# One reciprocal standard deviation for two lanes, in place of one per lane, in a four-layer token tower

## The reference

```python
h = tok(x, W)                              # rows of the table, 0 where the id is 0
h = h + attn0(_layernorm(h), ...)          # decayed linear attention
h = h + ffn0(_layernorm(h), ...)           # 16 experts, the best 2, then a layer norm with gamma, beta
h = h + attn1(_layernorm(h), ...)          # softmax over 8 positions, two heads
h = h + ffn1(_layernorm(h), ...)           # 32 experts, the best 1
h = h + attn2(_layernorm(h), ...)          # linear attention (elu), two layer norms, gelu
h = h + ffn2(_layernorm(h), ...)           # 8 experts, the best 2, gelu
h = h + attn3(_layernorm(h), ...)          # complex diagonal recurrence
h = h + ffn3(_layernorm(h), ...)           # binary gated weights

def _layernorm(x, axis=-1, eps=1e-05):
    m = jnp.mean(x, axis=axis, keepdims=True)
    v = jnp.var(x, axis=axis, keepdims=True)
    return (x - m) / jnp.sqrt(v + eps)
```

## Time and profile before

| | |
|---|---|
| runs | 1108.0, 1112.93, 1113.48 us; median 1112.93 |
| span of the profiled execution (first to last instruction) | 1110.5 us; a time of its own is not given |
| instructions | 12887 |
| pass one, pass two (first work of VectorE) | from 39.5 us, from 580.6 us |
| busy: TensorE matmul / weight load | 956.3 us (86%) / 686.4 us (62%) |
| busy: VectorE / ScalarE / GpSimd | 580.2 us (52%) / 362.3 us (33%) / 359.3 us (32%) |
| mean granted TensorE clock | 0.717 of full speed |
| DMA | 8.01 MB in 7687 packets, nearly all in the setup |

### The profile page before, as it was taken

The page is one execution under the profiler, slowest core; times in us unless marked ns, Lnnn a source line. Parts: engine busy times, 40 slices in busy tenths (PEclk is TensorE's granted clock), DMA queues, the critical chain, the costliest instruction groups (busy, mean ns, idle before and its releaser), DMA issues. The chain is left out here.

```text
span 1110.5 us, 12887 instructions
## 1 busy us (share of the span) xinstructions
PE 956.3 (86%) x4368; PEld 686.4 (62%) x4380; DVE 580.2 (52%) x1892; ACT 362.3 (33%) x654; POOL 359.3 (32%) x418
## 2 busy tenths in 40 slices
PE   0498999989996869979959899998999965997997
PEld 0276999776675537763316689987677643586332
DVE  6344226854226663467863622487421567427787
ACT  2115431121111332019941254211200222400896
POOL 6511347431101720476002114574110064028600
PEclk9999997555555557559975599865555555856898
DMA  6000000000000000001000000000000000000520
GB/s 174 9 1 1 1 1 1 1 1 0 1 1 1 1 1 1 0 1 20 1 22 1 0 1 1 1 1 1 1 1 1 0 1 0 1 1 1 14 6 20
DMA packets 7687, 8.01 MB, mean 7 GB/s; under 512 B 5513, under 2 KB 6122, under 8 KB 7466
## 3 DMA queue, kind: packets, MB, share of 16 engines
q0 software_dynamic: 1536, 1.58, 2.5%
q1 hardware_dynamic: 5746, 4.27, 1.5%
q10 hardware_dynamic: 336, 1.31, 0.4%
HBM read 5.90 MB, written 1.25 MB: 6 GB/s over the span
## 5 line engine op out<-in xcount | busy, mean ns | idle before, releaser
L626 POOL TENSOR_SCALAR var_eps<-stat 128x4 f32<-128x4 f32 x88 | 24.7, 280 | 498.3 <-DVE stat L1173 498.3
L942 PEld LDWEIGHTS psB<-k,hid 128*128 128x128 f32 x1024 | 127.8, 201 | 4.1
L844 ACT ACTIVATE hid<-psA 128x512 bf16<-128x512 f32 x256 | 126.0, 989 | 1.0 <-PE psA L1127 1.0
L942 PE MATMUL psB<-k,hid 128*128 128x64 f32 x1024 | 125.4, 282 | 0.0
L1494 DVE TENSOR_TENSOR hid<-hid 128x512 bf16<-128x512 bf16 x256 | 108.8, 426 | 18.4 <-ACT hid L844 2.5
L859 PE MATMUL psA<-kc,xn 128*64 128x128 f32 x256 | 60.4, 405 | 66.1 <-DVE xn L1184 66.0
L765 ACT ACTIVATE hid<-psA,k 128x512 f32<-128x512 f32 x128 | 79.9, 687 | 98.8 <-PE psA L869 98.7
L629 POOL TENSOR_TENSOR inv_std<-var_eps,neg_half 128x4 f32<-128x4 f32 x88 | 95.4, 1084 | 7.3
L868 PE MATMUL psA<-xs,up_hi 128*128 128x512 f32 x176 | 89.0, 506 | 2.9 <-DVE gTb L1374 1.1
L859 PEld LDWEIGHTS psA<-kc,xn 128*64 128x64 f32 x256 | 37.2, 161 | 85.7 <-DVE xn L1184 72.6
L1127 PE MATMUL psA<-gTb,w_rows 128*128 128x512 bf16 x252 | 85.3, 383 | 3.7 <-DVE gTb L1485 1.3
(11 more groups left out here) (269 smaller groups left out, 1756.9 us busy)
## 6 DMA issues: line engine op xcount, KB each, us to landing
hid<-wup SPq DMA_DIRECT2D x2, 512.0 KB, 11.4
out<-h SPq DMA_DIRECT2D x8, 128.0 KB, 1.9
k<-w ACTq DMA_DIRECT2D x1, 972.5 KB
hid<-binary SPq DMA_DIRECT2D x1, 608.0 KB
hid<-wup SPq DMA_DIRECT2D x2, 270.0 KB, 13.5
emb<-emb_w,ids_next POOLq DMA_INDIRECT x32, 3.4
kc<-consts SPq DMA_DIRECT2D x1, 384.5 KB, 7.4
emb<-emb_w,ids_sb POOLq DMA_INDIRECT x16, 5.3
```

Source lines behind the costliest of these rows:

```text
L844: act.activation(sg[l][:, p % 2, :], psA[l][:, :], ACT.Sign).then_inc(m3_s[g], 1)
L942: last = pe.matmul(psB[l][:, to:to + D], tile(hid[l][:, e % 4, :], t), k128[:, a:a + D], start=True, stop=True)
```

## The change

A group's eight variances get one add and one power on 128x8, where each lane's four had their own. The GpSimd step yields once, at the place that lane 1 had, waits for lane 1's `norm_var`, and counts each semaphore up by 2. VectorE's program is the same; its two multiplies still wait for the counts 1 and 2 of each norm, which now come together. `neg_half` gets eight columns.

```diff
@@ -208,7 +208,7 @@
         stat = per_group("stat", [P, GROUP_TILES, 2])
         var_eps = per_group("var_eps", [P, GROUP_TILES])
         inv_std = per_group("inv_std", [P, GROUP_TILES])
-        neg_half = sb("neg_half", [P, TILES])
+        neg_half = sb("neg_half", [P, GROUP_TILES])
@@ -620,14 +620,13 @@
                         def rstd(at, use):
 
-                            for l in own:
-                                yield at + RSTD + LATER * (l - own[0])
-                                pool.wait_ge(norm_var[g], nth(l, use))
-                                G.tensor_scalar(part(var_eps[g], l), part(stat[g], l)[:, :, 1], LN_EPS, None,
-                                                ALU.add).then_inc(norm_eps[g], 1)
-                                pool.wait_ge(norm_eps[g], nth(l, use))
-                                G.tensor_tensor(part(inv_std[g], l), part(var_eps[g], l), neg_half[:, :],
-                                                ALU.pow).then_inc(norm_rstd[g], 1)
+                            yield at + RSTD + LATER
+                            pool.wait_ge(norm_var[g], nth(own[-1], use))
+                            G.tensor_scalar(var_eps[g][:, :], stat[g][:, :, 1], LN_EPS, None,
+                                            ALU.add).then_inc(norm_eps[g], GROUP_LANES)
+                            pool.wait_ge(norm_eps[g], nth(own[-1], use))
+                            G.tensor_tensor(inv_std[g][:, :], var_eps[g][:, :], neg_half[:, :],
+                                            ALU.pow).then_inc(norm_rstd[g], GROUP_LANES)
```

## The result

| | before | after |
|---|---|---|
| median of the runs | 1113.2 us (4 runs, 1108.0 to 1127.54) | 1131.12 us (4 runs, 1126.98 to 1134.93) |
| ratio of the times, 95% interval | | 1.0157, 1.0102 to 1.0211 |
| span of the profiled execution | 1110.5 us | 1127.4 us |
| mean granted TensorE clock | 0.717 | 0.712 |

What follows compares the result with a forecast made beforehand. TensorE was busy 86% of the span, so GpSimd counted only by delay inside norms. Terms of 6.74 us a pass, +13.5 in two passes, on the 1112.93 median gave 1126.4 us; range 1109 to 1131, the forecast's own 1121 to 1131.

Steps and rivals of the forecast that it cites:

- P: Time of the joined power on 128x8: taken as 1.94 us, all work per element, with a low end of 1.08.
- The fixed-cost case: Rival: the power is mostly fixed cost, so P lies below 1.22 us; run about 1110.0 us; chance 0.22.
- my slope of 19 us per us: Predicted growth of the two-pass loss with P, 19 us per us, crossing nothing at P = 1.22.
- A0 of group 0: At this norm both lanes' transposes end later, at 587.94 instead of 587.20: +0.74 us a pass.
- M0 of group 1: At this norm the multiply, behind other VectorE work, starts at 627.28 instead of 627.09: +0.19 us a pass.
- A1 of group 0: At this norm the longer power delays GpSimd's expert sums by 0.87 us, making a later add late: +0.4 a pass.
- A1 of group 1 with M1 of group 0: Two norms: later multiply in the first, +0.66 us; later multiply, transposes and routing matmul in the second, +0.93.
- IN2 of group 1: Lane 1 aggregates 3.7 us after lane 0, then the longer power and lane 0's work delay transposes: +1.3 us a pass.
- M2 of group 1 with OUT2 of group 0: Second norm's VectorE multiply stands ahead of the first's lane 1 subtract, making it 1.36 us late: +1.2 a pass.
- The norms priced at nothing: The other norms, hidden behind VectorE or TensorE work: no cost, but up to 1.1 us each if cover is gone.
- Partly hidden: Rival: P is 1.5 us or TensorE's other group fills gaps; half the sum, 1119.7 us; chance 0.24.
- New waits: Rival: VectorE's queue passes on late multiplies and thin covers break, 3.6 to 5.4 us more, 1130 to 1132; chance 0.07.

Runs made afterwards that it cites:

- experiment 1: Kernel before with extra GpSimd powers of 1 to 64 columns and three multiplies in the setup; powers took 1636 ns on 8 columns, 10546 on 64.
- Experiment 10: Changed kernel with a multiply in place of the power, once per group, so outputs are not the reference's; 1095.2 us, ratio 0.978.
- Experiment 4: Changed kernel with the group's pair at lane 0's place in GpSimd's queue instead of lane 1's; 1156.63 us, ratio 1.0201.
- experiment 6: Covered grouping: changed kernel with the pair joined only at ten norms a pass predicted to cost nothing, old code at the other twelve; 1151.68 us, ratio 1.0102.
- 9: Kernel before with a multiply in place of each power, once per lane, so outputs are not the reference's; 1100.54 us, ratio 0.9899.
- 3: Kernel before with its two short add-and-power pairs kept, both held back until lane 1 is aggregated; 1135.78 us, ratio 1.003.
- Experiment 11: Long power per lane: kernel before with each lane's power done twice over its four values (128x8), no waiting for the other lane; 1152.19 us, ratio 1.0368.
- 12: Kernel before with the add of eps moved from GpSimd to VectorE, a repeat on another chip; 1110.27 us, ratio 0.9966.

## Why the prediction was right, and where it was not

The direction and the mechanism stood: slower, at a chance of 0.64, because a longer power ends later in front of the first multiply. The size, 1126.4 us forecast and 1131.12 measured, 13.5 us of loss against 18, came near partly by luck. The measured time stands 0.1 us above the end of the range that I gave, and in the sum errors of opposite sign met: the power was priced too high, while the start of the joint pair, one collision and the clock were not in it.

**P, the power on 128x8, was mis-sized.** I took 1.94, all work per element over a start of 0.22. It takes 1.67 as a rule; the source view of the line in after (min/median/max ns):

```profile
L628 POOL TENSOR_TENSOR inv_std<-var_eps,neg_half x44: 1665/1666/1963, 43.0 to 1048.0; 128x8 f32<-128x8 f32 x44
```

Between my ends, 1.08 and 1.94, I had gone to the upper one because I lent the power another operation's start. The fixed-cost case falls: experiment 1 shows 159 ns a column. By the Trainium skill, GPSIMD Engine Reference, section 3.1, a column would cost about 2.6 cycles; for this operation the measurement differs from it by far, and decides. By my slope of 19 us per us, P = 1.67 would give 19 x (1.67 - 1.22) = 8.6, a time of 1121.5.

**The joint pair also starts later, which I had put at nothing.** In most norms of after the add starts 0.16 us behind the aggregation and the power 0.39 behind the start of the add; before it was 0.09 and 0.31. Experiment 10 has the same 0.16 and 0.39 with a multiply, so it is not the power. These 0.15 us stand in front of every result. With them P is as good as 1.82, and the slope gives 11.4 us in place of 8.6. What causes them no run shows.

**The terms, us a pass, as predicted at P = 1.94 and as the marks show them:**

| term | predicted | shown (pass one / two) |
|---|---|---|
| A0 of group 0 | 0.74 | 0.76 / 0.72 |
| M0 of group 1 | 0.19 | 0.4 |
| A1 of group 0 | 0.4 | 1.28 / 1.28 |
| IN0 of group 1 | 0.37 | 0.45 / 0.47 |
| A1 of group 1 with M1 of group 0 | 0.66 + 0.93 | 1.1 / 1.3 |
| IN2 of group 1 | 1.3 | 0.91 / 0.93 |
| OUT2 of group 1 | 0.1 | 0.40 / 0.41 |
| M2 of group 1 with OUT2 of group 0 | 1.2 | 0.92 / 0.70 |
| M2 of group 0 | 0.1 | 0.17 / 0.17 |
| A3 of group 0 | 0.75 | 0.67 / 0.64 |
| sum | 6.74 | about 7.0 |

M0 of group 1 is read at its multiplies in pass two, since the clock touches the mark behind it.

*A0* was hit although P is smaller. From the add to the first multiply it takes 2.46 us in pass two, where I had 0.31 + 1.94 + 0.10 = 2.35: the power takes 1.96 there. In pass one the power takes 1.68, but the add in front of it 0.56 in place of 0.24. I had lane 0 at 1.1 later and lane 1 at 0.1; it was 1.30 and 0.55, and both lanes' transposes ended 0.73 later, as forecast. M0 of group 1 has a power of 1.91.

*A1 of group 0* is the step that failed. I had let the longer power push GpSimd's sums by 0.87 and counted 0.4 at the end of them. Timeline of after, pass two:

```profile
736.18 0.41 POOL L625 TENSOR_SCALAR var_eps<-stat 128x8 f32<-128x8 f32 x1
...
736.75 1.67 POOL L628 TENSOR_TENSOR inv_std<-var_eps,neg_half 128x8 f32<-128x8 f32 x1
737.02 0.41 DVE L1177 TENSOR_TENSOR xn<-h,stat 128x256 f32<-128x256 f32 x1
738.38 1.26 POOL L651 TENSOR_TENSOR big_c<-big_a,big_c 128x512 f32<-128x512 f32 x1
...
738.51 1.41 DVE L1183 TENSOR_TENSOR xn<-xn,inv_std 128x256 f32<-128x256 f32 x1 [1.08 <-POOL inv_std L628]
...
739.85 0.68 DVE L1301 TENSOR_TENSOR big_b<-psB,gate 128x512 f32<-128x512 f32 x1
...
740.61 2.60 POOL L651 TENSOR_TENSOR big_c<-big_b,big_c 128x512 f32<-128x512 f32 x2 [0.96 <-DVE big_b L1301]
```

Lane 0's multiply now starts 0.13 us behind GpSimd's sum and takes 1.41 us instead of 0.42: it ends at 739.92, 0.28 behind the end of the sum at 739.64, as if it had stood still until then. The Trainium skill, SBUF — State Buffer, section "SBUF: two separate sides", says that a VectorE operation with two SBUF inputs and a GpSimd operation that reads SBUF exclude each other for the whole instruction, and whoever starts second waits; this place agrees. A place 1.5 us earlier does not: VectorE's centring (L1177, two inputs) ran from 737.02 at its usual 0.41 us inside the power of 736.75, which took its usual 1.67. There the measurement decides. The multiply holds VectorE's product L1301, and GpSimd then stands idle 0.96 us for that product before its next two sums. I had followed GpSimd's queue and not asked what the moved multiply would run beside. 0.9 us more, in both passes. Experiment 4 bears this out: the multiply is as slow there (1.41), but two sums stand behind the power, so GpSimd has work and the idle time before the next pair of sums is gone; A1 of group 0 then costs 0.73 in place of 1.28.

*IN2* came as drawn, its size by the smaller P. From the start of the power to the first transpose it is 3.57 us in the earlier trace rows and 909.45 - 904.92 = 4.53 here:

```profile
904.92 1.67 POOL L628 TENSOR_TENSOR inv_std<-var_eps,neg_half 128x8 f32<-128x8 f32 x1
...
906.69 0.76 DVE L1183 TENSOR_TENSOR xn<-xn,inv_std 128x256 f32<-128x256 f32 x2 [1.68 <-POOL inv_std L628]
907.20 1.52 POOL L635 TENSOR_TENSOR aff<-xn,krow 128x256 f32<-128x256 f32 x2 [0.61 <-DVE xn L1183]
...
909.45 1.93 PE L858 MATMUL psA<-kc,aff 128*64 128x128 f32 x8 [8.17 <-POOL aff L638]
```

*M2 and OUT2* show the collision that the prediction described in the earlier trace rows. Timeline of after:

```profile
933.66 1.67 POOL L628 TENSOR_TENSOR inv_std<-var_eps,neg_half 128x8 f32<-128x8 f32 x1
933.79 0.68 DVE L1197 TENSOR_TENSOR xs<-psA,xs 64x512 fp32r<-64x512 f32 x1
...
935.43 0.87 DVE L1183 TENSOR_TENSOR xn<-xn,inv_std 128x256 f32<-128x256 f32 x1 [0.96 <-POOL inv_std L628]
...
936.33 0.68 DVE L1197 TENSOR_TENSOR xs<-psA,xs 64x512 fp32r<-64x512 f32 x1
```

VectorE stands idle 0.96 us in front of OUT2's multiply while lane 1's subtract, which TensorE wants, stands behind it until 936.33.

**The norms priced at nothing** show nothing in the marks of experiment 6.

**The rivals.** *Fixed cost* falls by experiment 1. *Partly hidden* falls for most terms on the chain: by the marks they landed whole, M2 with OUT2 excepted (0.92 and 0.70 of 1.2). *New waits* named the right kind of thing: the time, 1131.12, lies in its 1130 to 1132, just outside the forecast's range. What it got from the queue is one place, A1 of group 0, and I had named L1198 for it instead, whose share I had already counted.

**Length or wait?** My terms mixed the two, and the experiments part them only in part. Shown is that joining costs because the joined operation is long: with one of 0.2 us it costs some 1 us a pass by the marks and nothing by the times (9 and 10), with the power 7.0 a pass and 18 us in the run. With the two short powers kept, the wait alone costs 3.4 us by the times but 8 to 9 of the change's 14 by the marks (3), and no run says which is right. Experiment 11 has twice as many long powers as the change and so doesn't measure the length alone. How much of the loss is the power's length and how much the wait for lane 1 stays open.

## What to carry to other kernels

Joining two small instructions saves only their fixed part; with an operation whose time is mostly per element the first consumer waits for the sum, so split such work by consumer, and join only what waits for nothing that ends late. Before joining, look at what share of the instruction is its start: here 0.36 of 1.67 us, too little to pay for lane 0's delay. And when an instruction moves, ask for each of its consumers which engine will be working beside it at its new time.

## What the runs showed of the hardware that I had not expected

**The power on GpSimd** costs 0.36 us plus 159 ns for each fp32 column on 128 partitions, from 4 to 64 columns; the multiply beside it is near 0.2 us up to 8 columns. The very first power of one column took 2.10 us, the later ones 0.55; it is no price of every first power, since the first in the kernel before takes 1.07 like the others.

**Neighbours.** The same multiply of 128x256 on VectorE takes 0.42 us alone and 1.41 behind a GpSimd sum; the power took 1.67 in 40 of 44 cases and 1.87 to 1.96 in four, each time with VectorE operations beside it, but as busy a VectorE stood beside some of the 40 as well. What sets the four apart is not shown.

**TensorE's granted clock differs in the same stretch of the same work.** Windows of before, of its second profile on another chip, and of the long power per lane, all the stage behind M2 in pass two (columns: window, length, then busy us (instructions) of PE, PEld, DVE, ACT, POOL, then the granted clock, the DMA share, GB/s):

```profile
929.00:979.00 50.00, 43.55 (x178) 29.10 (x178) 23.64 (x83) 17.21 (x29) 4.42 (x8) 0.70 0.00 1
```

```profile
954.00:1018.00 64.00, 58.25 (x177) 36.32 (x178) 23.24 (x78) 17.51 (x29) 3.88 (x6) 0.50 0.00 1
```

```profile
945.00:1011.00 66.00, 58.36 (x178) 36.40 (x178) 23.96 (x84) 17.48 (x29) 5.67 (x7) 0.50 0.00 1
```

The same 178 matmuls take 50 us at 0.70 and 64 at 0.50, that is, at 1.2 GHz throughout, in one and the same kernel. The covered grouping and the long power drew the low level there, before drew both. So a single profile can hold 14 us that another execution of the same kernel doesn't have, nearly the size of what was measured here; the growths norm by norm separate the two, a comparison of spans doesn't. But the clock need not be chance alone: the four executions of the long power have a mean granted clock of 0.689 to 0.695, and none of the 23 of before on that chip is below 0.704. So part of the 41 us of experiment 11 seems to come by way of the clock. Whether later results make the low level likelier, which would explain why the timed losses of experiments 6 and 11 exceed their marks, stays open.

**Pauses of three engines at once.** On two of the three later chips the last expert stage has pauses, mostly of 1 to 3 us and of 4.3 at most, in which TensorE, VectorE and ScalarE all stand, in kernels of every kind. The waits of the kernel before in its second profile (columns as above):

```profile
ACT hid L844 <- remote: 14.3, 8, 2.9
DVE hid L1494 <- remote: 2.4, 1, 2.4
```

"Remote" is the profile's name for a releaser that it finds on no engine of this core; the first profile of before has no such wait. The first chip and the one of experiments 9 to 12 show none. What it was no run here tells.
